# Second layer of a decoder: the last three operations of a chain's first FP4 rounding of gated rows move from VectorE to GpSimd

## The reference, cut to what matters

```python
_GRID = [0.0, 0.5, 1.0, 1.5, 2.0, 3.0, 4.0, 6.0]; _MID = [0.25, 0.75, 1.25, 1.75, 2.5, 3.5, 5.0]
def fp4_quant_dequant(x):                      # blocks of 16 along the last dim
    scale = max(max|xb| / 6.0, 1e-12)
    idx = searchsorted(_MID, |xb / scale|)
    return _GRID[idx] * sign(xb) * scale
gate = fp4_linear(x, w_gate)                   # 256 -> 704
y = fp4_linear(x, w_up)                        # 256 -> 704
h = silu(gate) * y
return fp4_linear(h, w_down)                   # 704 -> 256, both operands rounded
```

## Time and profile before

| | us |
|---|---|
| median of 3 runs | 2876.49 (2875.19 to 2884.41) |
| the profiled execution | 2881.71 |
| its span | 2880.0 |
| VectorE busy | 2194.8 |
| TensorE busy | 2053.4 |
| ScalarE busy | 1748.7 |
| GpSimd busy | 652.8 |

### The profile page before, as it was taken

The page is one execution under the profiler, slowest core; times in us unless marked ns, Lnnn a source line. Parts: engine busy times, 40 slices in busy tenths (PEclk is TensorE's granted clock), DMA queues, the critical chain, the costliest instruction groups (busy, mean ns, idle before and its releaser), DMA issues. The chain is left out here.

```text
span 2880.0 us, 41500 instructions
## 1 busy us (share of the span) xinstructions
PE 2053.4 (71%) x11052; PEld 1159.4 (40%) x11052; DVE 2194.8 (76%) x10063; ACT 1748.7 (61%) x5698; POOL 652.8 (23%) x343
## 2 busy tenths in 40 slices
PE   6232555646556465555657599999999999799997
PEld 3122434434334343343444333334343343465554
DVE  5999999999999999999997355555555555276677
ACT  3678888888888888888881244444444444222221
POOL 0000000000000000000000166766767667200000
PEclk9555556555565555655555699999999999799999
DMA  5742222222222222222210000000000000201100
GB/s 113 152 103 49 50 69 52 55 56 66 49 52 59 63 55 49 58 64 52 55 33 4 4 13 12 13 16 16 11 13 16 15 13 12 88 8 45 41 11 8
DMA packets 86798, 123.55 MB, mean 43 GB/s; under 512 B 17444, under 2 KB 65224, under 8 KB 86600
## 3 DMA queue, kind: packets, MB, share of 16 engines
q1 hardware_dynamic: 86600, 121.37, 17.7%
HBM read 100.33 MB, written 21.00 MB: 42 GB/s over the span
## 5 line engine op out<-in xcount | busy, mean ns | idle before, releaser
L1494 ACT ACTIVATE mix_cand<-mix_pre,mixer_cbuf 128x32 f32<-128x32 f32 x2048 | 591.3, 289 | 166.0 <-DVE mix_pre L1424 82.3
L1491 ACT ACTIVATE mix_cand<-mix_state,mixer_cbuf 128x32 f32<-128x32 f32 x2048 | 652.9, 319 | 34.9 <-DVE mix_state L1416 4.5
L1411 DVE SCALAR_TENSOR_TENSOR mix_prod<-mixer_keys,mixer_cbuf,mix_cand 128x65 f32<-128x65 f32 x2048 | 581.7, 284 | 34.3 <-ACT mix_cand L1494 27.2
L1925 DVE TENSOR_REDUCE self_tops<-self_rough 128x2 f32<-128x1024 f32 x256 | 313.5, 1225 | 365.8 <-PE self_rough L1697 362.6
L1424 DVE SCALAR_TENSOR_TENSOR mix_pre<-mixer_keys,mix_gap,mix_state 128x32 f32<-128x32 f32 x2048 | 526.1, 257 | 27.8
L1523 PE MATMUL mix_out<-all_ident,mix_state 128*128 128x128 f32 x512 | 161.9, 416 | 488.6 <-ACT mix_flat L1475 432.5
L1416 DVE SCALAR_TENSOR_TENSOR mix_state<-mix_cand,mixer_cbuf 128x32 f32<-128x32 f32 x2048 | 507.6, 248 | 0.1
L1911 POOL TENSOR_TENSOR self_psum<-self_psum,self_prob 128x1024 f32<-128x1024 f32 x192 | 451.5, 2352 | 128.3 <-ACT self_prob L1838 118.7
L1838 ACT ACTIVATE self_prob<-self_sco 128x1024 f32<-128x1024 f32 x256 | 260.4, 1024 | 117.1 <-PE self_sco L1710 102.4
L875 POOL TENSOR_TENSOR mix_st_norm_rstd<-mix_st_norm_var,mix_half 128x2 f32<-128x2 f32 x24 | 16.7, 697 | 1316.4 <-DVE mix_st_norm_var L868 1316.4
L1523 PEld LDWEIGHTS mix_out<-all_ident,mix_state 128*128 128x128 f32 x512 | 82.4, 206 | 571.2 <-ACT mix_flat L1475 504.8
(11 more groups left out here) (386 smaller groups left out, 3273.7 us busy)
## 6 DMA issues: line engine op xcount, KB each, us to landing
mixer_keys<-k_rows SPq DMA_DIRECT2D x256, 260.0 KB, 4.9
aT_rows<-self_aT SPq DMA_DIRECT2D x32, 256.0 KB, 2.3
two_aT<-aT_rows SPq DMA_DIRECT2D x8, 1024.0 KB, 7.3
coef_rows<-mixer_coef SPq DMA_DIRECT2D x4, 1280.0 KB, 7.3
mixer_cbuf<-coef_rows SPq DMA_DIRECT2D x64, 80.0 KB, 5.5
k_rows<-mixer_krow SPq DMA_DIRECT2D x32, 65.0 KB, 5.0
proj_xin<-in_xT SPq DMA_DIRECT2D x8, 256.0 KB, 3.3
mix_st_xin<-in_x SPq DMA_DIRECT2D x8, 256.0 KB, 5.5
```

What stands on the lines that cost most here:

```text
L1411: dve.scalar_tensor_tensor(prod[:, b, :], keys[:, h, b, s_, :], coef(NIB, h, s_, b), cand[:, b, s % 2, :], ALU.mult, ALU.mult, accum_out=g ...
L1491: act.activation(cand[:, b, (s + 1) % 2, NS:2 * NS], state[:, hp, sp_, b, :], ACT.Copy, scale=cbuf[:, h, KEEP, b, s_:s_ + 1]).then_inc(kep ...
L1494: act.activation(cand[:, b, (s + 1) % 2, 0:NS], pre[b], ACT.Tanh, scale=cbuf[:, h, BETA, b, s_:s_ + 1]).then_inc(c_ready[b], 1)
L1925: dve.tensor_reduce(tops[:, kh, t, :], rough[:, :, :], AX.X, ALU.max).then_inc(rough_taken, 1)
```

## The change

For each chain the first hidden tile of a group is handled by two new functions. steps_dve (VectorE) does the product, the maxima, the scale into a tile of its own (ff_scale0), the reciprocal and the scaling, which now writes straight into hq; then the mask, and one instruction in place of L2083 that takes the maximum with 1 and multiplies by MAGIC, into a bf16 tile (ff_steps). round_pool (GpSimd) adds that tile to hq, takes it off again and multiplies by the scale repeated over each block of 16, three instructions on 128x704, each waiting for the one ahead. It runs in GpSimd's order after norm1 of the next group and ahead of norm3. Since steps_dve writes hq early, it waits at its head for the turns of the group before. The second hidden tile of a chain is rounded by quantise as before. TensorE's and ScalarE's orders stay as they are.

```diff
--- before.py
+++ after.py
@@ -2103,6 +2103,8 @@
         self.xq, self.xqT = sb("xq", [P, CTILES, D]), sb("xqT", [P, KT, GT])
         self.gate, self.h, self.hq, self.hqT = sb("gate", [P, FI]), sb("h", [P, FI]), sb("hq", [P, FI]), sb("hqT", [P, CTILES, self.FT, P])
         self.work = QuantiseRoom(sb("n", [P, FI]), sb("e", [P, FI]), *QuantiseRoom.small(ch.sb, "q", FI))
+        self.steps, self.scale0 = ch.sb("ff_steps", [P, FI], BF16), ch.sb("ff_scale0", [P, FI // BLK])
+        self.scaled, self.scaled_links, self.pool_links = ch.sem("ff_scaled"), ch.sem("ff_scaled_links"), ch.sem("ff_pool_links")
         self.xq_ready, self.x_flipped, self.xT_ready, self.gu_ready, self.gate_ready, self.h_ready = (
             sem("xq_ready"), sem("x_flipped"), sem("xT_ready"), sem("gu_ready"), sem("gate_ready"), sem("h_ready"))
         self.hq_ready, self.h_flipped, self.hT_ready, self.y_ready, self.x_links, self.h_links = (
@@ -2149,17 +2151,48 @@
         act.activation(self.gate[:, 0:self.SPLIT], banks[0][:, :], ACT.Silu)
         act.activation(self.gate[:, self.SPLIT:FI], banks[1][:, 0:self.REST], ACT.Silu).then_inc(self.gate_ready, 1)
 
-    def hidden_dve(self, dve, g, j):
-        link = ChainLinks(dve, self.h_links, Fp4Weights.QLINKS, g * CTILES + j)
-        banks = self.ch.banks
+    def product_dve(self, dve, g, j):
+        banks, up = self.ch.banks, self.SPLIT - self.REST
         dve.wait_ge(self.gate_ready, g * CTILES + (j + 1))
-        up = self.SPLIT - self.REST
         dve.tensor_tensor(self.h[:, 0:up], self.gate[:, 0:up], banks[1][:, self.REST:self.SPLIT], ALU.mult)
         dve.tensor_tensor(self.h[:, up:FI], self.gate[:, up:FI], banks[2][:, 0:FI - up], ALU.mult).then_inc(self.h_ready, 1)
+
+    def steps_dve(self, dve, g):
+
+        self.product_dve(dve, g, 0)
+        link = ChainLinks(dve, self.scaled_links, 5, g)
+        block = lambda a: a.rearrange("p (n c) -> p n c", c=BLK)
+        n, e, h, steps = block(self.hq[:, :]), block(self.work.e[:, :]), block(self.h[:, :]), block(self.steps[:, :])
+        amax, inv = self.work.amax[:, :], self.work.inv[:, :]
+        dve.wait_ge(self.h_ready, g * CTILES + 1)
+        if g > 0:
+
+            dve.wait_ge(self.h_flipped, g * self.PARTS)
+        alone(link(dve.tensor_reduce(amax, h, AX.X, ALU.max, apply_absolute_value=True)))
+        alone(link(dve.tensor_scalar(self.scale0[:, :], amax, 1.0 / 6.0, 1e-12, ALU.mult, ALU.max)))
+        alone(link(dve.reciprocal(inv, self.scale0[:, :])))
+        alone(link(dve.scalar_tensor_tensor(n, h, Fp4Weights.SHY, bcast(inv, 2, BLK), ALU.mult, ALU.mult)))
+        alone(link(dve.tensor_scalar(e.bitcast(I32), n.bitcast(I32), 0x7F800000, None, ALU.bitwise_and)))
+        dve.tensor_scalar(steps, e, 1.0, Fp4Weights.MAGIC, ALU.max, ALU.mult).then_inc(self.scaled, 1)
+        link.close()
+
+    def round_pool(self, pool, g):
+
+        block = lambda a: a.rearrange("p (n c) -> p n c", c=BLK)
+        n, steps = block(self.hq[:, :]), block(self.steps[:, :])
+        link = Links(pool, self.pool_links, 2, g)
+        pool.wait_ge(self.scaled, g + 1)
+        link(pool.tensor_tensor(n, n, steps, ALU.add))
+        link(pool.tensor_tensor(n, n, steps, ALU.subtract))
+        pool.tensor_tensor(n, n, bcast(self.scale0[:, :], 2, BLK), ALU.mult).then_inc(self.hq_ready, 1)
+        link.close()
+
+    def hidden_dve(self, dve, g):
+        link = ChainLinks(dve, self.h_links, Fp4Weights.QLINKS, g)
+        self.product_dve(dve, g, 1)
         yield
-        dve.wait_ge(self.h_ready, g * CTILES + (j + 1))
-        for ins, last in quantise(dve, self.work, self.hq[:, :], self.h[:, :],
-                                  (self.h_flipped, g * self.PARTS + 2 * j) if j > 0 else None):
+        dve.wait_ge(self.h_ready, g * CTILES + 2)
+        for ins, last in quantise(dve, self.work, self.hq[:, :], self.h[:, :], (self.h_flipped, g * self.PARTS + 2)):
             if last:
                 ins.then_inc(self.hq_ready, 1)
             else:
@@ -2400,6 +2433,8 @@
                     for c in chains:
                         c.norm1.pool(pool, g + 1)
                 for c in chains:
+                    c.ff.round_pool(pool, g)
+                for c in chains:
                     c.norm3.pool(pool, g)
 
         @block.vector
@@ -2432,11 +2467,11 @@
                 for c in chains:
                     alone(c.round_dve(dve, g))
                 next_norm(one, g)
-                alone(one.ff.hidden_dve(dve, g, 0))
+                one.ff.steps_dve(dve, g)
                 next_norm(two, g)
-                alone(two.ff.hidden_dve(dve, g, 0))
-                alone(one.ff.hidden_dve(dve, g, 1))
-                alone(two.ff.hidden_dve(dve, g, 1))
+                two.ff.steps_dve(dve, g)
+                alone(one.ff.hidden_dve(dve, g))
+                alone(two.ff.hidden_dve(dve, g))
                 alone(one.norm3.dve(dve, g))
                 last = two.norm3.dve(dve, g)
             alone(last)
```

## The result

Median 2886.15 us of 20 runs (2878.54 to 2894.80), against 2877.68 us of 20 runs of the kernel before on the same chips: ratio 1.0023, interval 1.0014 to 1.0033 (the quotient of the two medians alone is 1.0029, inside the interval). The change costs 6.6 us (4.0 to 9.5). Measured once more beside the last experiments it was 1.0017 (1.0005 to 1.0028).

The account below looks back on a forecast made before the run. VectorE was taken to set the time in each group's first half, TensorE behind the seam. Three groups at -0.2 us (-0.5) and the last at -0.9 gave -1.4 us, a 2875.1 us median; range 2871.5 to 2896.

Parts of the forecast that it names:

- The port: VectorE reading two SBUF tensors beside GpSimd's six instructions per group: neither waits, so nothing is charged.
- the first rival: "Each waits for the other's instruction, by turns": VectorE and GpSimd alternate on SBUF reads; +8.4 us, 2884.9 us, chance 0.25.
- VectorE does get the 2.66 us: Groups 1 to 3: chain two's norm and product start 2.66 us earlier on VectorE, the gate being there.
- gaps before VectorE's two-input instructions: Sign the forecast is wrong: such gaps on VectorE; TensorE's wait at the seam then grows to 4 us and more.
- The term for GpSimd's instruction: Each 128x704 tensor_tensor on GpSimd estimated at 1.67 us, bounded by 1.26 and 2.35 us.
- T: One rounding on GpSimd: three instructions of 1.67 us and two semaphore hops of 0.07 us, 5.15 us.
- the seam: Where TensorE waits 1.1 us for chain two's two_ff_hq; VectorE's gain counts only there, 0.2 us per group.
- the steps on VectorE: L2083's replacement taking max and product and writing bf16: 0.53 us taken, 0.89 the upper bound.
- The last group: No norm1 in between: down starts 0.4 us later, a 1.3 us TensorE wait goes, net -0.9 us.

Follow-up runs that it names:

- e1: Kernel before plus a measuring stretch behind its last norm, twelve VectorE forms without and beside GpSimd; tensor_tensor of two SBUF inputs on 704 elements 0.89 to 1.54 us.
- e3: Changed kernel with GpSimd's three operations of chain one's rounding on the first 16 columns only; ratio 0.9982, 5.2 us faster than before.
- e2: Kernel before with two more 128x704 VectorE products ahead of the last operation of chain two's first rounding in each group; ratio 1.0034, 9.8 us slower.
- e4: Changed kernel, but GpSimd starts chain one's rounding only when chain two's norm1 has been applied; ratio 1.0023 to the kernel before.
- e6: Half of the change: GpSimd finishes chain one's first rounding only, chain two's is whole on VectorE; ratio 0.9993 to the kernel before.
- e7: Kernel before, no GpSimd work added, chain two's next norm1 behind chain one's second rounding, its TensorE turns behind chain one's last down products; 0.9988, 3.5 us faster.
- e5: Kernel of e2 with one more 128x44 product; single execution, the 24 down matmuls took 7.67, 7.04 and 7.04 us.
- e8: Changed kernel with e7's order on VectorE and TensorE, chain two's norm1 behind both roundings on GpSimd too; ratio 0.9988, 3.5 us faster than before.

## Why the prediction was wrong, step by step

The forecast was no change, -1.4 us, with its range from 2871.5 to 2896 us for a median of 2876.49; the run became 6.6 us slower.

- **The step that failed is "The port"**: the forecast charged nothing for VectorE and GpSimd reading side by side. It rested on the earlier trace rows, a power on 32 elements. e1 shows that this power indeed stops nobody, while a tensor_tensor on 704 elements held up all four tried forms with two SBUF inputs and all three of tensor_scalar from SBUF, by 0.53 to 0.65 us, until it ended. In the changed kernel this brought chain two's steps 2.28 us later than forecast, and the clock fell behind the longer wait (below). The row was weak evidence, as the text said, and was still given the largest chance.
- **The place was missed even by the first rival, and its number is luck.** "Each waits for the other's instruction, by turns" gave +8.4 us; 6.6 were measured, 9.6 in the trace. But none of its terms took place: GpSimd never waited in the changed kernel, and chain two's steps were not stretched (4.59 us, 4.63 forecast). It counted two-input instructions only, and the costliest collision is L510, a tensor_scalar with one tensor input, right where chain one's rounding starts on GpSimd: 2.45 us in each of three groups. So the forecast's "VectorE does get the 2.66 us" held for 0.34 us: chain two's product starts 8.84 us behind the start of gate_up, for 9.18 before and 6.52 forecast, and its steps end 13.43 us behind it, where the forecast has 2577.10 - 2565.95 = 11.15. The sign it named, gaps before VectorE's two-input instructions, could not show this either, as the wait lies inside the instructions.
- **The term for GpSimd's instruction was too dear**: 1.52, 1.52 and 1.38 us for 1.67, a rounding 4.57 us for T = 5.15. That gave 0.6 us back in each group; two_ff_hq was ready 18.08 us behind the start of gate_up, where the forecast has 16.35 and the kernel before 16.55.
- **The clock was left out.** Of the 10.3 us of the three groups 5.7 came from it. No text of the prediction has it: neither the forecast nor a rival asked what TensorE does after a longer wait. It was put at nothing without a reason, and in the trace it is the larger part.
- **Right:** the seam as the place that decides, and the steps on VectorE (L2176 takes 0.53 us). e3 shows the seam's value: with VectorE's 2.66 us really free (and chain one's GpSimd work left out), the run is 5.2 us faster and no more, out of 21.3 us taken away. The last group, where no norm1 lies, came as forecast: two_ff_hq 1.8 us late (1.6 forecast), the group 0.7 us shorter (0.9).
- **The Trainium skill's rule** (SBUF — State Buffer, section Who interferes with whom), that a VectorE instruction with two SBUF inputs, or in its two-port mode, and a reading GpSimd instruction exclude each other for the whole instruction, agrees with e1 for 704 elements, and not for the power on 32. The same section says that an instruction with at most one SBUF input, outside the two-port modes, does not contend; in e1 the reduction, the reciprocal and the statistics kept their lengths.
- **L510 fits that rule too, by its price.** It takes 0.41 us for 256 elements, as much as tensor_scalar from PSUM (0.42), and waited all the same (0.94 in e1). But it reads two scalars by pointer, and the kernel before shows what these cost on 16 elements, with pointers (L1207, from PSUM) and without (L403):

```profile
L1207 DVE TENSOR_SCALAR mix_st_z<-mix_bank,mix_st_emv,mix_st_erstd x16: 286/290/295, 404.1 to 1586.1; 128x16 f32<-128x16 f32 x16
...
L403 DVE TENSOR_SCALAR proj_nrm<-proj_nrm x4: 167/169/169, 38.2 to 84.9; 128x16 f32<-128x16 f32 x4
```

From 290 ns on 16 elements to 410 ns on 256 is 0.50 ns per element. tensor_scalar from SBUF with constants (L2083, 427 ns on 512 and 527 on 704) has 0.52, a two-input instruction (L2084, 693 and 893 ns) 1.04. So, as an estimate, L510 runs at the halved price of L2083 plus some 0.12 us for its pointers. No run isolated that.

**Still open:** what decides whether the clock falls. At the seam it did not fall behind waits of 0.4 to 1.5 us, nor at 2.96 us in three groups of e2; at 2.97 to 2.99 it fell in nine of nine (the changed kernel twice, e4), at 3.20 in three of three, and at 2.12 us behind light work in two of three. At the last down product of the run it fell behind waits of 1.19 (e6), 1.27 (e7), 2.39 (e5) and 2.40 us (e2), and did not behind 1.28 us in the kernel before. So the length of the wait alone tells it at neither place. What part of the measured 6.6 us is the clock, outside the profiled executions, was not measured either.

## What to carry to other kernels

Before moving work from VectorE to GpSimd, look at what VectorE does meanwhile. In these runs inputs from PSUM, reductions, reciprocals and statistics did not wait; count every tensor_scalar from SBUF and every instruction with two SBUF inputs as stopped to the end of the GpSimd instruction. An average of busy time (76% and 23%) says nothing of this, and neither do GpSimd instructions that read little. Placing the work well removed the loss (e8), but no run shows that the move itself gained time: e8 was no faster than e7, the same order with no work moved. So ask first at the seam what the work is late for: here an order that moved one norm got 3.5 us.

## What the runs showed of the hardware that I had not expected

- VectorE's wait for GpSimd lies inside the instruction's recorded length, not ahead of it: L2078 on 44 elements shows 1.43 us instead of 0.19. Look for a longest duration far over the form's median.
- A tensor_tensor of 128x704 on GpSimd took 1.67 us with two f32 inputs (e1), 1.52 with one in bf16, and 1.38 where one is a 44-element scale repeated 16 times.
- In the changed kernel GpSimd's instructions never grew (1515 to 1527 ns), although VectorE was waiting at the ends of four of the six in each of the first three groups (L510 twice, L2078, L2080); in e1 GpSimd waited 0.57 us where VectorE had started first.
- TensorE's granted clock of 0.50 outlasted the wait by some 6 us in the first group, with matmuls running without a break. In the second group it was still 1.00 when TensorE went on at 2676.07, fell about 1 us later and stayed low for 3.4 us (0.54 over 2677 to 2680, 0.66 over 2680 to 2681).
- The same fall came at the run's last down product behind 1.19 us of waiting in one kernel (e6) and did not behind 1.28 us in another.
